# Centring the weights of a pre-norm attention and spiking-FFN layer on TensorE, and four instructions moved on VectorE

## What is computed

```
x = x + attn(layernorm(x))
    Q, K, V = x wq^T, x wk^T, x wv^T          (64 wide)
    out = (Q (K^T V)) * sqrt(3/64) wo^T       (per batch)
x = x + ffn(layernorm(x))
    h = relu(x W_fc^T)^2                      (1024 wide)
    y = h W_proj^T
    five steps of mem = 0.9 mem + y - (mem > 1); count how often mem > 1
    result = count / 5
```

## Time and profile before

| | us |
|---|---|
| median of 3 runs | 485.45 |
| the runs | 482.1, 485.59, 485.45 |
| the profiled execution | 485.44 |
| its span, first to last instruction | 483.4 |
| TensorE busy | 459.1 |
| VectorE busy | 364.7 |
| ScalarE busy | 281.1 |
| GpSimd busy | 237.9 |

### The profile page before, as it was taken

One profiled execution on the slowest core, in us unless ns is written; L12 is line 12 of the kernel. 1 busy time (PEld: TensorE's weight loads), 2 busy tenths in 40 slices (PEclk: granted clock), 3 DMA queues, 4 the chain that ended last, 5 costly groups with the idle time before them and its releaser, 6 DMA issues. The chain is left out here.

```text
span 483.4 us, 8236 instructions
## 1 busy us (share of the span) xinstructions
PE 459.1 (95%) x2856; PEld 409.2 (85%) x2856; DVE 364.7 (75%) x924; ACT 281.1 (58%) x519; POOL 237.9 (49%) x197
## 2 busy tenths in 40 slices
PE   7599899999999999999989999999999999999993
PEld 6478689898989889898979989898988889898993
DVE  4667648879887868878786888889787886758457
ACT  3338656756665755756665575766667475656530
POOL 1236635474655455564653556555554643444430
PEclk9989989999999999999998999999999999999998
DMA  8510304262352424253341424425142404130011
GB/s 300 123 45 25 64 0 133 43 171 50 87 132 66 126 72 130 45 154 64 79 128 57 130 45 113 106 77 130 57 96 44 125 1 103 45 90 38 34 45 43
DMA packets 120969, 41.29 MB, mean 85 GB/s; under 512 B 114016, under 2 KB 114656, under 8 KB 120672
## 3 DMA queue, kind: packets, MB, share of 16 engines
q1 hardware_dynamic: 120928, 40.78, 32.9%
HBM read 25.03 MB, written 15.73 MB: 84 GB/s over the span
## 5 line engine op out<-in xcount | busy, mean ns | idle before, releaser
L389 POOL TENSOR_TENSOR hid_l<-hid,hid_h 128x512 fp32r<-128x512 f32 x128 | 166.7, 1303 | 201.7 <-ACT hid_h L444 201.6
L431 ACT ACTIVATE relu<-hid_ps 128x512 f32<-128x512 f32 x128 | 76.5, 598 | 125.9 <-PE hid_ps L893 124.7
L892 PE MATMUL y_ps<-wdn_l,hid_h 128*128 128x256 f32 x480 | 136.6, 285 | 0.0
L893 PE MATMUL y_ps<-wdn_h,hid_l 128*128 128x256 f32 x480 | 136.5, 284 | 0.0
L891 PE MATMUL y_ps<-wdn_h,hid_h 128*128 128x256 f32 x480 | 136.1, 284 | 0.0
L891 PE MATMUL hid_ps<-x2T_h,wup_h 128*128 128x512 f32 x256 | 106.1, 415 | 5.5 <-DVE x2T_l L701 5.5
L892 PE MATMUL hid_ps<-x2T_l,wup_h 128*128 128x512 f32 x256 | 101.2, 395 | 0.0
L893 PE MATMUL hid_ps<-x2T_h,wup_l 128*128 128x512 f32 x256 | 100.5, 393 | 0.0
L770 DVE SCALAR_TENSOR_TENSOR cnt<-y_ps,bound,cnt 128x256 f32<-128x256 f32 x240 | 98.2, 471 | 0.2
L891 PEld LDWEIGHTS y_ps<-wdn_h,hid_h 128*128 128x128 f32 x480 | 92.5, 193 | 5.2
L892 PEld LDWEIGHTS y_ps<-wdn_l,hid_h 128*128 128x128 f32 x480 | 92.4, 193 | 4.9
(11 more groups left out here) (135 smaller groups left out, 577.3 us busy)
## 6 DMA issues: line engine op xcount, KB each, us to landing
xs<-x_dram SPq DMA_DIRECT2D x15, 512.0 KB, 4.6
out_dram<-x SPq DMA_DIRECT2D x15, 512.0 KB, 2.6
x_blocks<-x SPq DMA_DIRECT2D x56, 128.0 KB, 2.7
x_block<-x_blocks SPq DMA_DIRECT2D x14, 512.0 KB, 3.6
x_block<-x_dram SPq DMA_DIRECT2D x104, 64.0 KB, 2.6
hid<-w_up_dram SPq DMA_DIRECT2D x1, 1024.0 KB, 7.1
x<-w_down_dram SPq DMA_DIRECT2D x1, 1024.0 KB, 9.2
xs<-x_dram SPq DMA_DIRECT2D x2, 256.0 KB, 2.9
```

The source lines that it names most:

```text
L389: nc.gpsimd.tensor_tensor(hid_l[:, i % 2, c, :], hid[:, c % 4, :], hid_h[:, i % 2, c, :].bitcast(f32), ALU.subtract).then_inc(hid_ready, 1)
L431: nc.scalar.activation(relu[:, c % 2, :], hid_ps[c % 2][:, :], ACT.Relu).then_inc(relu_done, 1)
L892: mm(dst, a[0], b[1], start=False, stop=False)
L893: return mm(dst, a[1], b[0], start=False, stop=stop)
```

## The change

1. `averager` goes. GpSimd makes `minus_mean` (all -1/256) and `centre` = identity + `minus_mean`, with one addition of 128 x 128. TensorE multiplies raw weights with `centre` (own chunk) and `minus_mean` (other chunk) and so has the centred weight in PSUM: w_kv and w_q in y_ps[0] and e_ps, w_up in four blocks of 512 columns in hid_ps[0], hid_ps[1], kv_ps and e_ps. Four small products per weight for two, eight of 512 columns for w_up instead of four.
2. High halves (ScalarE) and low halves (VectorE, w_up's too) are taken from PSUM. VectorE's centring instructions and GpSimd's low halves of w_up go. In the start the order of ScalarE, VectorE and TensorE changes: project_q behind the energy sum's first part, blocks of w_up between them, keep_warm(3) becomes 2, keep_warm(2) and keep_warm(4) go, w_down's second high half moves into ScalarE's chunk 1 of step 0.
3. Step 0: TensorE does project_kv(0, 3) after chunk 5 instead of 6 and its turn after 6 instead of 7; ScalarE's kvT_out(0, 3) moves with it; GpSimd's inverse_deviation for group 3 comes before chunk 6 instead of at the end; VectorE does first_moments(0, 3) ahead of x2T_low_half(0, 1), and moments(0, 1) last.
4. Every step: VectorE does turn_blocks behind q_low_half and energy_sum, and x2T_low_half ahead of the second half of spikes(i - 1, bank 0).

```diff
@@ gpsimd
-            nc.gpsimd.memset(averager[:, :], 1.0 / EMB).then_inc(averager_ready, 1)
+            nc.gpsimd.memset(minus_mean[:, :], -1.0 / EMB).then_inc(minus_mean_ready, 1)
...
+            nc.gpsimd.tensor_tensor(centre[:, :], ident[:, :], minus_mean[:, :], ALU.add).then_inc(centre_ready, 1)
...
-            low_half_of_up(0)
-            low_half_of_up(1)
@@ gpsimd step
-                    if c == (1 if is_first(r, i) else 4) and there(r, i + 3):
-                        inverse_deviation(r, 2 if is_first(r, i) else i + 3)
+                    if c == 4 and there(r, i + 3) and not is_first(r, i):
+                        inverse_deviation(r, i + 3)
+                    if is_first(r, i) and c in (1, 6):
+                        inverse_deviation(r, 2 if c == 1 else 3)
...
-                if is_first(r, i):
-                    inverse_deviation(r, 3)
@@ scalar, start
             kv_high_half(0, 0)
-            q_high_half(0, 0)
             kvT_out(0, 1)
             high_half_of_up(0)
             kv_high_half(0, 1)
+            q_high_half(0, 0)
+            energy_first_half(0, PER_BATCH - 1)
             q_high_half(0, 1)
-            energy_first_half(0, PER_BATCH - 1)
-            half_of_columns(w_loaded["down"], wdn_raw, wdn_h, wdn_high, 0)
             eo_high_half(0, PER_BATCH - 1)
             high_half_of_up(1)
-            half_of_columns(w_loaded["down"], wdn_raw, wdn_h, wdn_high, 1)
+            half_of_columns(w_loaded["down"], wdn_raw, wdn_h, wdn_high, 0)
+            high_half_of_up(2)
+            high_half_of_up(3)
             x2T_high_half(0, 0)
@@ vector
+            def low_half_of_up(b):
+
+                dve.wait_ge(wup_high, b + 1)
+                k, cols = up_columns(b)
+                nc.vector.tensor_tensor(wup_l[:, k, cols], up_block(b), as_f32(wup_h[:, k, cols]), ALU.subtract).then_inc(wup_ready, 1)
...
-            def centre_up(h, k):
-
-                dve.wait_ge(wup_mean, h + 1)
-                rows = wup_raw.rearrange("p (k n) -> p k n", k=EC)[:, k, h * HID // 2:(h + 1) * HID // 2]
-                nc.vector.tensor_tensor(rows, rows, hid_ps[h][:, :], ALU.subtract).then_inc(wup_centred, 1)
@@ vector first_step
                 kv_low_half(0, 2)
+                first_moments(0, 3)
                 x2T_low_half(0, 1)
-                first_moments(0, 3)
-                moments(0, 1)
                 kv_scale(0, 3)
                 kv_low_half(0, 3)
+                moments(0, 1)
@@ vector step
-                if there(r, i + 3):
-                    turn_blocks(i + 3)
                 if there(r, i + 2):
                     q_low_half(r, i + 2)
                 if there(r, i + 2) and closes_batch(i + 2):
                     energy_sum(r, i + 2)
+                if there(r, i + 3):
+                    turn_blocks(i + 3)
...
+                if there(r, i + 1):
+                    x2T_low_half(r, i + 1)
                 if there(r, i - 1):
                     spikes(r, i - 1, 0, range(PAIR_OPS // 2, PAIR_OPS))
-                if there(r, i + 1):
-                    x2T_low_half(r, i + 1)
@@ vector start
-            centre_weights(w_loaded["kv"], wkv_raw[:, :], 0, wkv_centred)
-            centre_weights(w_loaded["qq"], wqq_raw[:, :], 1, wq_centred)
             first_moments(0, 0)
...
             kv_scale(0, 0)
-            centre_up(0, 0)
             kv_low_half(0, 0)
             kv_scale(0, 1)
-            centre_up(0, 1)
+            low_half_of_up(0)
             kv_low_half(0, 1)
...
-            centre_up(1, 0)
-            centre_up(1, 1)
+            low_half_of_up(1)
             residual(0, 0)
             x2T_low_half(0, 0)
+            low_half_of_up(2)
+            low_half_of_up(3)
@@ tensor
+            def centre_up(b, part):
+
+                k, cols = up_columns(b)
                 rows = wup_raw.rearrange("p (k n) -> p k n", k=EC)
...
+                done = mm(up_block(b), (centre if part == k else minus_mean)[:, :], rows[:, part, cols],
+                          start=(part == 0), stop=(part == EC - 1))
@@ tensor first_step
+                    if c == 5:
+                        project_kv(0, 3)
                     if c == 6:
                         energy_sum(0, 2)
-                        project_kv(0, 3)
-                    if c == 7:
                         turn_kv(0, 3)
@@ tensor start
-            keep_warm(3)
+            keep_warm(2)
             project_kv(0, 0)
-            project_q(0, 0)
+            centre_up(0, 0)
             turn_kv(0, 0)
             project_kv(0, 1)
-            average_up(0)
-            project_q(0, 1)
+            centre_up(0, 1)
             turn_kv(0, 1)
             energy_sum(0, 0)
+            project_q(0, 0)
+            centre_up(1, 0)
             energy_sum(0, 1)
-            keep_warm(2)
+            project_q(0, 1)
             energy_times_wo(0, PER_BATCH - 1)
-            average_up(1)
+            centre_up(1, 1)
+            centre_up(2, 0)
             attend(0, 0)
-            keep_warm(4)
+            centre_up(2, 1)
+            centre_up(3, 0)
+            centre_up(3, 1)
             turn_x1(0)
```

More of the change, by code:

```diff
@@ L132, in build, with small_centred, up_block, up_columns @@
         e_ps = bank("e_ps")
+        def small_centred(which):
+            return (y_ps[0], e_ps)[which][:, 0:2 * EC * HEAD].rearrange("p (k n) -> p k n", k=EC)
+        def up_block(b):
+            return (hid_ps[0], hid_ps[1], kv_ps, e_ps)[b][:, :]
+        def up_columns(b):
+            return b % EC, slice(b // EC * HID // 2, (b // EC + 1) * HID // 2)
         def by_matmul(r, n):
@@ L414, in _, with high_half_of_kv, high_half_of_q @@
         def _(act):
-            def high_half_of_weights(centred, raw, high, out_high):
-                act.wait_ge(centred, 1)
-                nc.scalar.activation(high[:, :, :], raw, ACT.Copy).then_inc(out_high, 1)
+            def high_half_of_kv():
+                act.wait_ge(wkv_centred, 1)
+                nc.scalar.activation(wkv_h[:, :, :], small_centred(0), ACT.Copy).then_inc(wkv_high, 1)
+            def high_half_of_q():
+                act.wait_ge(wq_centred, 1)
+                nc.scalar.activation(wq_hl[:, :, 0, :], small_centred(1)[:, :, 0:HEAD], ACT.Copy).then_inc(wq_high, 1)
             def half_of_columns(loaded, raw, high, out_high, h):
@@ L523, in first_step @@
                         xT_high_half(0, 3)
+                    if c == 1:
+                        half_of_columns(w_loaded["down"], wdn_raw, wdn_h, wdn_high, 1)
                     if c == 2:
@@ L563, in step @@
                     high_half(r, i, FC - 1)
[L566 to L568 removed]
+            high_half_of_kv()
+            high_half_of_q()
             xT_high_half(0, 0)
@@ L593, in _, with low_half_of_kv, low_half_of_q @@
                 nc.vector.memset(credit[:, 1 + n:2 + n], 0.0).then_inc(s, 16)
[L594 to L605, removed]
+            def low_half_of_kv():
+                dve.wait_ge(wkv_high, 1)
+                nc.vector.tensor_tensor(wkv_l[:, :, :], small_centred(0), as_f32(wkv_h[:, :, :]), ALU.subtract).then_inc(wkv_ready, 1)
+            def low_half_of_q():
+                dve.wait_ge(wq_high, 1)
+                nc.vector.tensor_tensor(wq_hl[:, :, 1, :], small_centred(1)[:, :, 0:HEAD], as_f32(wq_hl[:, :, 0, :]),
+                                        ALU.subtract).then_inc(wq_ready, 1)
+            def low_half_of_up(b):
+                dve.wait_ge(wup_high, b + 1)
+                k, cols = up_columns(b)
+                nc.vector.tensor_tensor(wup_l[:, k, cols], up_block(b), as_f32(wup_h[:, k, cols]), ALU.subtract).then_inc(wup_ready, 1)
             def kv_scale(r, n):
@@ L915, in turn_first, with centre_weights @@
                 last.then_inc(first_x_turn, 1)
-            def average_weights(loaded, raw, first):
+            def centre_weights(loaded, raw, which, done):
                 pe.wait_ge(loaded, 16)
+                w = raw.rearrange("p (k n) -> p k n", k=EC)
                 for k in range(EC):
-                    last = mm((y_ps[0], e_ps)[first][:, 0:2 * HEAD], averager[:, :], raw[:, k * 2 * HEAD:(k + 1) * 2 * HEAD],
-                              start=(k == 0), stop=(k == EC - 1))
-                last.then_inc(mean_done, 1)
+                    for j in range(EC):
+                        last = mm(small_centred(which)[:, k, :], (centre if j == k else minus_mean)[:, :], w[:, j, :],
+                                  start=(j == 0), stop=(j == EC - 1))
+                last.then_inc(done, 1)
             def turn_x1(n):
@@ L933, in turn_x1 @@
                 last.then_inc(first_x1_turn, 1)
-            def average_up(h):
-                pe.wait_ge(w_loaded["up"], 16)
-                pe.wait_ge(xT_ready, 2)
+            def centre_up(b, part):
+                k, cols = up_columns(b)
                 rows = wup_raw.rearrange("p (k n) -> p k n", k=EC)
-                for k in range(EC):
```

(19 more changed lines are left out.)

39 lines of the change are left out of this document (15 added, 24 removed).

## The result

The changed kernel takes 472.74 us (median of four runs, 470.9 to 473.47) against 485.29. The ratio is 0.9752, with a 95% interval of 0.9709 to 0.9794. The forecast was 475.4, range 469.5 to 480.5.

What follows compares the result with a forecast made beforehand. TensorE was taken as the bound, busy 459 of 483.4 us. 483.4 - 7.5 - 1.0 - 1.4 - 3.6 - 1.3 + 4.8 = 473.4, with 2.0 around the span 475.4; range 469.5 to 480.5.

Steps and rivals of the forecast that it cites:

- Start: Up to the first project_up: it starts at 28.5 instead of 36.03 us, gain 7.5, bounds 5.5 to 8.5.
- Steps 0 and 1: The 2.42 us gap at 61.57 and its half clock go, smaller new gaps come; net gain 1.0.
- Borders: Between steady steps: the wait on x2T_l goes, a y-bank gap of 0.2 comes; 0.13 at 11 borders, 1.4 won.
- The late border: Border at 252.84 with late DMA: its 1.95 us gap and 1.7 of half-clock loss go, 3.6 won.
- The last stretch: Last two step borders (0.3 and 0.5 idle) lose their gaps; 1.3 won.
- Batch-closing steps: Six steps where later VectorE work makes TensorE wait at energy_times_wo and attend; loss 2.2 to 7.5, taken as 4.8.
- The rule of the Trainium skill: GpSimd and VectorE contend for SBUF; alone it takes the 7.5 loss in batch-closing steps, total about 478.
- Loops win in full: Steady steps: neither y's bank nor eo_l holds TensorE, so 467.3; chance 0.14.
- Start wins less: Start or first steps: the clock falls again near 30 or 50 us, about 480; chance 0.16.
- no net change: New late events replace the one at 252.84 and the start gains 5.5: 481 to 486; chance 0.07.
- Slower: Batch-closing steps: VectorE's lateness at attend idles TensorE about 2 us and drops its clock, about 493; chance 0.05.

Runs made afterwards that it cites:

- d_step0_old: The changed kernel with step 0's old order on all four engines; 472.07 us.
- after_again: The changed kernel run once more, unchanged, for a second profile; 473.32 us.
- b: The kernel before the change with only VectorE's new order in steps 1 to 16; 479.69 us, 0.9886 of before.
- c: The changed kernel with turn_blocks ahead of q_low_half and energy_sum again, x2T_low_half left early; 479.02 us.
- f_counts_first: The changed kernel with the four counts that free y's bank put ahead of x2T_low_half on VectorE; 469.66 us.
- h: g with step 0 reordered: project_kv(0,3) after chunk 6 again, group 3's rstd and kv high half earlier; 465.23 us.
- j_late_eo: The changed kernel with 0.67 us of unused VectorE work ahead of eo_low_half in batch-closing steps; 477.49 us.
- g: f_counts_first with ScalarE's high halves of x1 ahead of kv's high half in chunk 6; 467.73 us.
- a: The changed kernel with VectorE's old order in steps 1 to 16; 478.36 us, 0.9858 of before.
- e_pool_waits: The kernel before the change with GpSimd's first low half of w_up held until kv's second low half is made; 481.6 us.
- k: The kernel before the change with 44 identity turns filling TensorE's gap ahead of the second energy sum; 482.08 us.

## Why the prediction was right, step by step

- **Start: 7.5 forecast, 6.75 measured.** The products cost what was worked out: three of w_up's start at 23.59, 24.45 and 25.31, 0.86 apart. No clock fell. Of the 0.75 that is missing, some 0.2 are there at the first project_kv already (10.24, forecast 10.05; x's second half landed later, TensorE waited 0.27 for it), 0.6 at turn_x1 (26.17, forecast 25.6), the rest at x1's low halves. Each link was a little longer than I put it.
- **Steps 0 and 1: 1.0 forecast, 1.45 measured.** The energy product stands 29.0 us into the steps, forecast 29.4, before 30.45. The new gap before project_kv was 1.59 (1.4 forecast), those at the energy sum and the product 0.66 and 0.24. That the sum held is in part luck, as the account of why it gains failed: d_step0_old has the old order and is not slower. The gain counted on the half clock behind the old gap, which came in four profiles with the old start and not in d's.
- **Borders: right.** x2T_l doesn't start 2.7 us earlier but when ScalarE allows, VectorE idles 2.26 for it (2.25 forecast), and the loss moves to y's bank: 0.17, forecast as 0.2. The gain is smaller than forecast: a step is 27.05 or 27.45 us long in turn, before 27.12 or 27.52 where nothing else disturbed it, so a border gives 0.07 and not 0.13. Some borders of before had longer waits (0.29 at 168.81), which go as well.
- **The late border: right.** Its gap never came back with the early low half (after, after_again, b, c, d, f, h, j; g has one wait of 0.53 at 241), and came back in a, without the half clock. From the energy product of step 1 to the opening of step 13 the span shrank by 4.96, where the borders (1.4) and the late one (3.6) were to give 5.0. The last stretch, forecast 1.3, gave 1.1.
- **Batch-closing steps: the term that was mis-sized.** 4.8 us were taken for them, the middle between 2.2 and 7.5. The profile of after has none, after_again 2.8 for three hits. The lower end was wrong: from turn_blocks on, the six counts and eo_l took 2.54 us, where the sum had 2.9 as in the earlier trace rows, whose pair of x-from-cnt took 1.03 and now takes 0.75; so eo_l comes 0.19 before attend and not 0.24 behind it. The upper end assumed a parted pair in every such step; it is parted ahead of none of the six (after) or of three (after_again). When it is, the cost is 0.95, forecast 1.25: with its restart the energy product costs 0.5, as forecast, attend another 0.46 and not 0.8. So the 4.8 stand against nothing in one profile and 2.8 in the other. It is the only term that was off by more than 0.8, and nearly all of the 2.7 us between forecast and median lie in it, as far as two profiles can say.
- **The rule of the Trainium skill** ("GPSIMD Engine Reference", section 1: the SBUF interfaces are shared with VectorE, whose instructions with two SBUF inputs contend for them). e_pool_waits and the 0.75 and 1.85 of the pair agree with it. Taken alone it would have given about 478: it says that the two contend, not how often a pair is really parted: here ahead of none or three of six such steps.
- **Rivals.** "Loops win in full" (467.3): half of its mechanism is there in the profiled run (470.9), where eo_l holds nothing up; the other half isn't, as y's bank does hold TensorE. "Start wins less" and "no net change" didn't come: the start won 6.75, no clock fell in it, and no late border took the place of the old one. "Slower" needed 2.5 us per batch-closing step; even j_late_eo, with 0.67 us of VectorE work more, shows waits of 0.36 to 0.83 there, in steps 0.63 to 1.59 longer.

## What to carry to other kernels

When an instruction is moved ahead, look at what it waits for: here its input came 2.3 us later than its new place, the engine idled, and all behind it was late. Fill such idle time with the instructions that somebody waits for (the four counts that free a bank) and keep the ones that nobody waits for behind; that was worth another 3.7 us, beside the 5 of the move itself. And where a margin is as small as here (0.19 us at attend) or an order is settled within some hundredths, a forecast can only give both outcomes: better to design such a place out, as f_counts_first does.

## What the runs showed of the hardware

- A GpSimd instruction and a pair of VectorE instructions with both inputs in SBUF, which come within a few hundredths of a microsecond, settle their order differently from run to run: the same pair at the same place takes 0.75 or 1.85 us.
- A short wait of TensorE costs more than the profile shows: 0.42 us of waits made a step 0.95 longer (after_again), one of 0.36 made it 0.63 longer (j).
- Idle time of TensorE does not bring its clock down by a fixed rule of length that these profiles show: it went to half (1.2 GHz) behind gaps of 1.95, 2.0, 2.4 and 3.1 us and within one of 4.8 (before, b, e, k), and stayed at 2.4 GHz after 2.19 (a) and 2.55 (d). The price of a gap of some 2 to 3 us is therefore itself, or itself plus the 1.7 that 3.4 us at half clock cost, and a forecast should carry both.
